# Middle mixture one expert further ahead, with two sum buffers and no loop, and the attention's mixture copied by VectorE

## The chip, the cores and the metric

The kernel runs on one core of one Trainium2 chip. The metric is the device time of one execution in microseconds, as the median over repeated runs of the same program; three runs of the kernel before are shown.

## What is computed

Sixteen sequences of 512 tokens with 256 features go through four blocks, each with a layer norm ahead of it and a residual around it: a linear-memory attention (layer 0), a mixture of eight routed experts and one shared expert (layer 0, the *middle mixture*), a windowed attention that is mixed with a state-space path and followed by an MLP (layer 1), and a top-1 mixture (layer 1). The change touches the second and the third:

```
# layer 0, mixture: 4 of 8 experts by grouped top-k, plus a shared expert
g = einsum('nh,ehi->eni', x, Wg);  u = einsum('nh,ehi->eni', x, Wu)
y = einsum('eni,eih->enh', silu(g) * u, Wd)
out = einsum('enh,ne->nh', y, cw) + mlp(x, Wg_s, Wu_s, Wd_s)
# layer 1, attention: gated sum of two products
x1 = x + g * (ao @ WO + bO) + (1 - g) * (states @ Cw)
```

Nothing of what is computed changes.

## The kernel before, in words

The program is written engine by engine: each engine has its own instruction list in program order, and engines meet at semaphores alone. The four blocks run one after another with a barrier between them. Matrix products are done in three parts (high x high, high x low, low x high halves; `three`, L70 to L74), so every operand of TensorE exists as a rounded high half and a remainder.

**Middle mixture** (`moe_phase`, L77, `shared=True`; its tiles are called `b_...`). A turn of the schedule is one expert of one sequence; nine experts make a sequence. In turn `e` TensorE does `down(e)` (L498: 12 matmuls of 256 columns into `y_ps`, one buffer) and then `gate_up(e + AHEAD)` (L486: 12 matmuls of 512 columns into one of the two slots of `gu_ps`), with `AHEAD = 2` (L86). Turns 2 and 3 have the transposes and the router of the next sequence as well. `down(e)` waits for the low half of `h` of expert `e` and for VectorE's sum of expert `e-1`, since `y_ps` has one buffer (two halves of it are signalled apart). `gate_up` waits until the slot that it overwrites was multiplied.

ScalarE's turn: `h_hi_copy(e)` (L254), `silu(e+1)` (L246), then parts of the next sequence. VectorE's turn: `h_lo_sub(e)` (L384), `accumulate(e-1)` (L392, four additions into the sum `acc`), `times_up(e+1)` (L375), then an extra part of the next sequence, by expert: 0 `stats_of` (L297), 1 `normalise` (L307), 4 `best_groups` (L332), 5 `lo_sub` (L370), 6 `ranks` (L316), 7 `weights_top4` (L345). The sum of the last expert ends the body. GpSimd only computes one inverse deviation per sequence.

SyncE's queue, per sequence `it` (L187 to L197): wait, load sequence `it+1` into the other half of `x_in`, wait for the whole sum of `it`, store `acc`. So the load of a sequence stands behind the store of the sequence two before it. `acc` has one buffer (L112); the first sum of a sequence waits for the store of the one before (L398).

`steps` (L56) runs the first and the last sequence as straight code and the fourteen between them in a hardware loop of seven turns of two sequences; there the values of waits and the DMA addresses come from registers.

**Layer-1 attention** (`attn1_phase`, L1306; tiles `c_...`) is straight code for all sequences. Per sequence 32 steps `n` run as a pipeline: scores (TensorE), `maxima` (VectorE, L1864), `exp` (ScalarE), inverse sums (VectorE), `normalise` (GpSimd), transposes (TensorE), `pT_copy` (ScalarE), values (TensorE). After each eight steps the product of a quarter is formed by `mix(it, t)` (L2115) in the PSUM tile `c_ps`, and `mix_copy(it, t)` (L1693, ScalarE) copies it to `mixed`, from which GpSimd builds `x1` in five parts (L1593 on). `mix(t+1)` and the next sequence's `state_input` (L2062) wait for that copy, because `c_ps` is one buffer. ScalarE's copies stand at `n` = 18, 26 and 34 and after the loop.

Of the kernel before, what the change touches and what calls it, by code (L numbers as in the profile page):

```python
# [51 lines left out]
def first_step(it):  # L52
    return isinstance(it, int) and it == 0


def steps(eng, body):  # L56

    body(0, 0)
    with eng.Fori(0, NSEQ // 2 - 1) as turn:
        body(turn * 2 + 1, 1)  # L60
        body(turn * 2 + 2, 0)
    body(NSEQ - 1, 1)


def sequence(v, it):
# [11 lines left out]
def moe_phase(nc, name, src, dst, wg_d, wu_d, wd_d, gate_d, bias_d, lower_d, half_d, ident_d, shared):  # L77
# [5 lines left out]
    NT = 1 if shared else 2  # L83
    YB = T * D // SEQ
    BT = T // YB
    AHEAD = 2  # L86
    src_v = src.rearrange("(n t p) d -> n p t d", t=T, p=P)
    dst_v = dst.rearrange("(n t p) d -> n p t d", t=T, p=P)
    with ExitStack() as ctx:
# [19 lines left out]
        eps = sb("eps", [P, T])  # L109
        ident = sb("ident", [P, P])  # L110
        x_in = sb("x_in", [P, 2, T, D])
        acc = sb("acc", [P, T, D])  # L112
        xn = sb("xn", [P, T, D])
        xT = sb("xT", [P, DC, SEQ])
        xT_hi = sb("xT_hi", [P, 2, DC, SEQ], F32R)
# [44 lines left out]
        hlo_ready = sem("hlo_ready")  # L160
        y_ready = sem("y_ready")
        acc_done = sem("acc_done")
        stored = sem("stored")
        dve_order = sem("dve_order")
        pool_order = sem("pool_order")
        LOADS = 8 if shared else 7
# [7 lines left out]
        @block.sync  # L174
        def _(sp):
            sp.dma_start(x_in[:, 0], src_v[0]).then_inc(x_loaded, 16)
            sp.dma_start(wgu_raw[:, 0, :], wg_d.rearrange("p e c i -> p (e c i)")).then_inc(loaded, 16)
            sp.dma_start(wgu_raw[:, 1, :], wu_d.rearrange("p e c i -> p (e c i)")).then_inc(loaded, 16)
            sp.dma_start(wd_raw[:], wd_d.rearrange("p e d -> p (e d)")).then_inc(loaded, 16)
            sp.dma_start(gate[:], gate_d).then_inc(loaded, 16)  # L180
            sp.dma_start(lower[:], lower_d).then_inc(loaded, 16)
            sp.dma_start(half[:], half_d).then_inc(loaded, 16)
            sp.dma_start(ident[:], ident_d).then_inc(loaded, 16)
            if shared:
                sp.dma_start(bias[:], bias_d).then_inc(loaded, 16)

            def body(it, par):  # L187

                if not last_step(it):

                    sp.wait_ge(var_ready, it + 1)
                    if not first_step(it):
                        sp.wait_ge(acc_done, (it - 1) * T * E + T)
                    sp.dma_start(x_in[:, 1 - par], sequence(src_v, it + 1)).then_inc(x_loaded, 16)

                sp.wait_ge(acc_done, (it + 1) * T * E)
                sp.dma_start(sequence(dst_v, it), acc[:]).then_inc(stored, 16)  # L197

            steps(sp, body)
            sp.wait_ge(stored, 16 * NSEQ)  # L200

        @block.gpsimd
        def _(pool):
# [14 lines left out]
        def _(act):  # L218
# [49 lines left out]
                evacuate(0, 1)  # L268
            hi_copy(0, 0)
            silu(0, 0, 0)  # L270

            def body(it, par):
                for e in range(E):
                    h_hi_copy(it, par, e)
                    if e + 1 < E:
                        silu(it, par, e + 1)
                    elif not last_step(it):
                        silu(it + 1, 1 - par, 0)
                    if not last_step(it):
                        if e == 2:  # L280
                            evacuate(it + 1, 0)
                        if e == (3 if shared else 4):
                            scores(it + 1)
                        if e == (4 if shared else 5):
# [7 lines left out]
        def _(dve):  # L292
# [99 lines left out]
            def accumulate(it, par, e):  # L392
                for t in range(T):
                    if t % BT == 0:
                        dve.wait_ge(y_ready, (it * E + e) * YB + t // BT + 1)

                    if e == 0 and t == 0 and not first_step(it):
                        dve.wait_ge(stored, it * 16)  # L398

                    if e and t == 0:  # L400
                        dve.wait_ge(acc_done, (it * E + e) * T)
                    into = x_in[:, par, t, :] if e == 0 else acc[:, t, :]
                    if e < E0:
                        nc.vector.tensor_tensor(acc[:, t, :], y_ps[:, t, :], into, ALU.add).then_inc(acc_done, 1)
                    else:
                        nc.vector.scalar_tensor_tensor(acc[:, t, :], y_ps[:, t, :], cw[:, par, t, e - E0:e - E0 + 1], into, ALU.mult, ALU.add).then_inc(acc_done, 1)  # L406

            stats_of(0, 0)
            normalise(0, 0)
# [11 lines left out]
                weights_top1(0, 0)  # L421
            lo_sub(0, 0)
            times_up(0, 0, 0)

            def body(it, par):
                order.step(it)
                for e in range(E):
                    h_lo_sub(it, par, e)
                    if e:
                        accumulate(it, par, e - 1)  # L430
                    if e + 1 < E:
                        times_up(it, par, e + 1)
                    elif not last_step(it):
                        times_up(it + 1, 1 - par, 0)
                    if not last_step(it):
                        if e == 0:
                            stats_of(it + 1, 1 - par)
# [868 lines left out]
def attn1_phase(nc, x, out, wqk_d, wvg_d, bw_d, cw_d, wo_d, w1_d, w2_d, spread_d, cols_d, rows_d, b1_d, a_d, window_d, half_d, ident_d):  # L1306
# [7 lines left out]
    with ExitStack() as ctx:  # L1314
# [325 lines left out]
        def _(act):  # L1640
# [49 lines left out]
                after(act, pv_done, G - 1)  # L1690
                nc.scalar.copy(pT[:, n % 2, :, b[0]:2], t_ps[:, n % 2, :, b[0]:2]).then_inc(pT_ready, 1)  # L1691

            def mix_copy(it, t):  # L1693
                act.wait_ge(mix_in_psum, it * T + t + 1)
                after(act, x1_done, it * T + t)
                nc.scalar.copy(mixed[:], c_ps[:]).then_inc(mix_copied, 1)

            def ao_hi(it, t):
                act.wait_ge(pv_done, it * NS + (t + 1) * PAIRS1)
                after(act, mix_in_psum, it * T + t)  # L1700
# [39 lines left out]
            def body(it):  # L1740
                q4_copy(it, HELD)
                for n in range(NS + LAG_T):
                    if HELD + 1 + n < PAIRS1:
                        q4_copy(it, HELD + 1 + n)
                    if n < NS:
                        exp(it, n)
                    if n >= LAG_T:
                        pT_copy(it, n - LAG_T)
                    if n in (13, 21, 29):
                        ao_hi(it, (n - 13) // 8)  # L1750
                    if n == 10:
                        state_hi(it)
                    if n in (18, 26, 34):
                        mix_copy(it, (n - 18) // 8)
# [5 lines left out]
                mix_copy(it, T - 1)  # L1760
                if not last_step(it):
                    projections(it + 1)

# [20 lines left out]
        def _(dve):  # L1784
# [87 lines left out]
            def inverse_sums(it, n):  # L1872
                dve.wait_ge(exp_ready, it * NS + n + 1)
                after(dve, norm_ready, it * NS + n - 3)
                nc.vector.reciprocal(inv[:, n % 4], psum[:, n % 4]).then_inc(inv_ready, 1)  # L1875

            def ao_lo(it, t):
                dve.wait_ge(aohi_ready, it * T + t + 1)
                nc.vector.tensor_tensor(aoT_hl[1][:], oT[t], aoT_hl[0][:].bitcast(F32), ALU.subtract).then_inc(aolo_ready, 1)
# [55 lines left out]
            def body(it):  # L1935
# [3 lines left out]
                for n in range(NS + 1):  # L1939
# [894 lines left out]
```

## Time and profile before

| | us |
|---|---|
| median of 3 runs | 4768.33 |
| the three runs | 4777.87, 4767.22, 4768.33 |
| the profiled execution, its own time | 4779.36 |
| its span in the trace | 4777.4 |
| its mean granted clock of TensorE | 0.95 |

The profiled execution is 11 us above the median, and 2 us of its time lie outside the traced span. The middle mixture runs from about 1840 to 2659 us of the span and the layer-1 attention from about 2660 to 4415 us. Times in rows are from the start of the span. In the trace PE is TensorE's matmul, PEld its weight load, DVE is VectorE, ACT ScalarE, POOL GpSimd, SPq the queue of SyncE; L406 is line 406. Matmuls overlap: the end shown of one is later than the start of the next, so "idle" is counted from a modelled end.

### The profile page before, as it was taken

What the parts mean: (1) busy time and instruction counts of PE and PEld (TensorE: products, weight loads), DVE (VectorE), ACT (ScalarE), POOL (GpSimd) and SP (SyncE); (2) the same over time, 40 slices, a digit from 0 to 9 for tenths busy, and PEclk for the clock granted to TensorE, in tenths of its full rate; (3) what the DMA queues carried; (4) which work ended last, traced back from release to release, by engine and by line L of the source; (5) the groups of instructions that cost most, each with busy time, mean ns of one, the idle gap of its engine ahead of it and who ended that gap; (6) DMA issues with size and microseconds to landing.
All of it is one profiled execution on the core that took longest, in us unless ns stands there. A gap on an engine that the chain in (4) does not pass through costs nothing. (4 is left out here: it accounts for less than half of the span.)

```text
span 4777.4 us, 147918 instructions
## 1 busy us (share of the span) xinstructions
PE 4059.4 (85%) x60532; PEld 3227.1 (68%) x60628; DVE 2999.0 (63%) x7236; ACT 2449.4 (51%) x5553; POOL 2220.0 (46%) x2255
## 2 busy tenths in 40 slices
PE   3888898888888885888888599999999999998668
PEld 2776677677767775777777366666676666666656
DVE  2777777777776775777777555555555555554455
ACT  3545555555555442333333366666666666666335
POOL 4666666666666650000000155555554555555354
PEclk8999999999999997999999799999999999999669
DMA  2222222221222121000000211111111111110233
GB/s 82 56 48 57 67 48 52 66 60 46 53 67 58 44 48 49 27 18 18 27 18 22 78 28 28 28 28 28 28 31 31 46 28 28 28 28 23 101 125 111
DMA packets 173293, 221.53 MB, mean 46 GB/s; under 512 B 32349, under 2 KB 117472, under 8 KB 171232
## 3 DMA queue, kind: packets, MB, share of 16 engines
q1 hardware_dynamic: 166160, 195.49, 15.5%
q0 software_dynamic: 6480, 16.92, 1.0%
q8 instruction: 461, 7.55, 0.7%
q14 instruction: 192, 1.57, 0.1%
HBM read 68.35 MB, written 44.19 MB: 24 GB/s over the span
## 5 line engine op out<-in xcount | busy, mean ns | idle before, releaser
L1591 POOL TENSOR_TENSOR c_prob<-c_prob,c_inv 128x512 f32<-128x512 f32 (+1 forms) x512 | 482.6, 947 | 648.8 <-DVE c_inv L1875 639.1
L1680 ACT ACTIVATE c_prob<-c_s_ps,c_nmax 128x256 f32<-128x256 f32 (+1 forms) x1024 | 459.2, 464 | 156.6 <-DVE c_nmax L1870 155.3
L1870 DVE TENSOR_REDUCE c_nmax<-c_s_ps 128x2 f32<-128x512 f32 (+1 forms) x512 | 316.8, 619 | 265.9 <-PE c_s_ps L2080 263.6
L848 POOL TENSOR_TENSOR a_swap<-a_swap,a_sin 128x512 f32<-128x512 f32 x128 | 204.9, 1600 | 533.0 <-DMA a_swap<-a_raw 533.0
L212 POOL TENSOR_TENSOR b_var<-b_mv,b_eps 128x4 f32<-128x4 f32 x16 | 8.5, 533 | 696.6 <-DVE b_mv L304 696.5
L889 ACT COPY a_raw<-a_w_ps 128x512 f32<-128x512 f32 x256 | 150.3, 587 | 332.1 <-PE a_w_ps L74 331.7
L1691 ACT COPY c_pT<-c_t_ps 128x512 f32<-128x512 f32 (+1 forms) x512 | 280.5, 551 | 50.0 <-PE c_ab_ps L2112 49.9
L2092 PE MATMUL c_t_ps<-c_ident,c_prob 128*128 128x128 f32 x1792 | 284.6, 275 | 21.8 <-ACT c_pT L1691 16.1
L1170 PE MATMUL a_w_ps<-a_mem,a_sT 64*32 64x65 f32 x14848 | 216.1, 226 | 94.7 <-issue 91.2
L2092 PEld LDWEIGHTS c_t_ps<-c_ident,c_prob 128*128 128x128 f32 x1792 | 214.5, 141 | 101.4 <-POOL c_prob L1591 36.2
L2080 PE MATMUL c_s_ps<-c_k,c_q 128*128 128x512 f32 (+1 forms) x512 | 272.6, 532 | 3.5 <-ACT c_prob L1680 3.5
L252 ACT ACTIVATE b_s_sb<-b_gu_ps 128x512 f32<-128x512 f32 x144 | 86.1, 598 | 368.9 <-PE b_gu_ps L74 368.9
L1170 PEld LDWEIGHTS a_w_ps<-a_mem,a_sT 64*32 64x32 f32 x14848 | 170.2, 106 | 146.2 <-issue 125.1
L72 PE MATMUL b_y_ps<-b_wd_hi,b_h_hi 128*128 128x256 f32 x576 | 176.6, 307 | 94.4 <-DVE b_acc L406 47.3
L72 PE MATMUL a_w_ps<-a_xT_hi,a_wqk_hi 128*128 128x512 f32 x512 | 233.3, 456 | 20.2 <-DVE a_x_ln L968 12.2
L1911 DVE TENSOR_TENSOR c_hT_lo<-c_ff,c_hT_hi 128x512 fp32r<-128x512 f32 x128 | 88.6, 692 | 248.6 <-ACT c_hT_hi L1725 248.6
L72 PE MATMUL b_gu_ps<-b_xT_hi,b_wgu_hi 128*128 128x512 f32 x576 | 234.1, 406 | 10.7 <-DVE b_xT_lo L373 10.7
L73 PE MATMUL b_gu_ps<-b_xT_hi,b_wgu_lo 128*128 128x512 f32 x576 | 232.9, 404 | 0.0
L74 PE MATMUL b_gu_ps<-b_xT_lo,b_wgu_hi 128*128 128x512 f32 x576 | 230.2, 400 | 0.0
L1680 ACT ACTIVATION_READ_ACCUMULATOR c_prob<-c_s_ps,c_nmax 128x1 f32 x1024 | 223.0, 218 | 0.0
L73 PE MATMUL a_w_ps<-a_xT_hi,a_wqk_lo 128*128 128x512 f32 x512 | 216.9, 424 | 3.0 <-issue 3.0
L74 PE MATMUL a_w_ps<-a_xT_lo,a_wqk_hi 128*128 128x512 f32 x512 | 215.9, 422 | 3.0 <-issue 3.0
(407 smaller groups left out, 13508.9 us busy)
## 6 DMA issues: line engine op xcount, KB each, us to landing
a_swap<-a_raw SPq DMA_DIRECT2D x1024, 64.0 KB
c_k<-c_aoT_hi SPq DMA_DIRECT2D x86, 128.0 KB, 2.4
c_k<-c_aoT_lo SPq DMA_DIRECT2D x86, 128.0 KB, 2.4
c_k<-c_stage SPq DMA_DIRECT2D x84, 128.0 KB, 2.3
d_xb<-sorted_rows SPq DMA_DIRECT2D x71, 130.0 KB
a_x_ln<-x SPq DMA_DIRECT2D x128, 64.0 KB, 2.1
a_acc<-x SPq DMA_DIRECT2D x64, 128.0 KB
after_attn<-a_acc SPq DMA_DIRECT2D x64, 128.0 KB, 2.5
```

What stands on the lines that cost most here:

```text
L72: nc.tensor.matmul(out, w[0], x[0], start=start, stop=False, **options)
L73: nc.tensor.matmul(out, w[1], x[0], start=False, stop=False, **options)
L74: return nc.tensor.matmul(out, w[0], x[1], start=False, stop=stop, **options)
L848: nc.gpsimd.tensor_tensor(q_sw, q_sw, table(sin), ALU.mult)
L889: (rawq_ready, rawk_ready)[a].by(nc.scalar.copy(raw[:, m % 3, a], bank))
L1170: ins = nc.tensor.matmul(into[s * SEG:(s + 1) * SEG, r, j], sT[d, (n // T * T + j) % (2 * PU), a, tok], mem[d, s, j], start=True, stop=True)
L1591: nc.gpsimd.tensor_tensor(p, p, inv[:, n % 4].unsqueeze(2).to_broadcast([P, 2, KB])[:, :, keys_of(i)], ALU.mult).then_inc(norm_ready, 1)
L1680: last = nc.scalar.activation(prob[:, n % 4, h, keys_of(i)], s_ps[:, n % 2, h, keys_of(i)], ACT.Exp, bias=nmax[:, n % 4, h:h + 1], accum_o ...
L1691: nc.scalar.copy(pT[:, n % 2, :, b[0]:2], t_ps[:, n % 2, :, b[0]:2]).then_inc(pT_ready, 1)
L1870: nc.vector.tensor_reduce(nmax[:, n % 4], s_ps[:, n % 2, :, keys_of(i)], AX.X, ALU.max, negate=True).then_inc(max_ready, 1)
L2080: last = nc.tensor.matmul(s_ps[:, n % 2, :, keys_of(i)], q4[:, j, i * P:(i + 1) * P], k4[:, j, :, keys_], start=False, stop=True, skip_gro ...
L2092: last = nc.tensor.transpose(t_ps[:, n % 2, h, b], prob[:, n % 4, h, b * P:(b + 1) * P], ident[:])
```

## The change

In the middle mixture experts run three ahead in TensorE's order. ScalarE's and VectorE's turn `e` handles the high and low half of expert `e+1` and the activation and product of expert `e+2`; VectorE adds the sum of `e-1` ahead of them. The sum has two buffers, each with a store semaphore of its own, and the sixteen sequences are written out as straight code. (`moe_phase` is called once, for this block.)

```
-    body(0, 0)
-    with eng.Fori(0, NSEQ // 2 - 1) as turn:
-        body(turn * 2 + 1, 1)
-        body(turn * 2 + 2, 0)
-    body(NSEQ - 1, 1)
+    for it in range(NSEQ):
+        body(it, it % 2)
...
-    AHEAD = 2
+    AHEAD = 3
...
-        acc = sb("acc", [P, T, D])
+        acc = sb("acc", [P, 2, T, D])
...
-                sp.dma_start(sequence(dst_v, it), acc[:]).then_inc(stored, 16)
+                sp.dma_start(sequence(dst_v, it), acc[:, par]).then_inc(stored[par], 16)
...
             def body(it, par):
                 for e in range(E):
-                    h_hi_copy(it, par, e)
-                    if e + 1 < E:
-                        silu(it, par, e + 1)
-                    elif not last_step(it):
-                        silu(it + 1, 1 - par, 0)
+                    for stage, later in ((h_hi_copy, e + 1), (silu, e + 2)):
+                        if later < E:
+                            stage(it, par, later)
+                        elif not last_step(it):
+                            stage(it + 1, 1 - par, later - E)
...
-                    if e == 0 and t == 0 and not first_step(it):
-                        dve.wait_ge(stored, it * 16)
+                    if e == 0 and t == 0 and it >= 2:
+                        dve.wait_ge(stored[par], it // 2 * 16)
...
                 for e in range(E):
-                    h_lo_sub(it, par, e)
                     if e:
                         accumulate(it, par, e - 1)
-                    if e + 1 < E:
-                        times_up(it, par, e + 1)
-                    elif not last_step(it):
-                        times_up(it + 1, 1 - par, 0)
+                    for stage, later in ((h_lo_sub, e + 1), (times_up, e + 2)):
+                        if later < E:
+                            stage(it, par, later)
+                        elif not last_step(it):
+                            stage(it + 1, 1 - par, later - E)
```

In the layer-1 attention `mix_copy` moves from ScalarE's list to VectorE's, at `n` = 18 and 26 and, after the loop, around the last low half:

```
-            def mix_copy(it, t):
-                act.wait_ge(mix_in_psum, it * T + t + 1)
-                after(act, x1_done, it * T + t)
-                nc.scalar.copy(mixed[:], c_ps[:]).then_inc(mix_copied, 1)
...
+            def mix_copy(it, t):
+                dve.wait_ge(mix_in_psum, it * T + t + 1)
+                after(dve, x1_done, it * T + t)
+                nc.vector.tensor_copy(mixed[:], c_ps[:]).then_inc(mix_copied, 1)
...
+                    if n in (18, 26):
+                        mix_copy(it, (n - 18) // 8)
...
+                mix_copy(it, T - 2)
                 ao_lo(it, T - 1)
                 if more:
                     qk_lo(it + 1, 0, 1)
+                mix_copy(it, T - 1)
                 stats2_of(it, T - 2)
```

## Rows read from the trace of the kernel before

**Rows 1.** Busy us of PE, PEld, DVE, ACT, POOL by stretch; clock, DMA share, GB/s.

```profile
1884.00:2656.00 772.00, 676.64 (x3793) 577.24 (x3792) 557.91 (x1643) 240.18 (x361) 23.43 (x30) 0.97 0.07 20
2740.00:4370.00 1630.00, 1522.85 (x10526) 1112.57 (x10619) 896.87 (x2074) 1083.96 (x3134) 876.90 (x1044) 1.00 0.12 30
```

**Rows 2.** Groups by line, 1884 to 2656 us: busy, mean ns, idle before and releasers.

```profile
L72 PE MATMUL b_y_ps<-b_wd_hi,b_h_hi 128*128 128x256 f32 x576 | 176.6, 307 | 94.4 <-DVE b_acc L406 47.3 <-DVE b_acc L404 39.6 <-DVE b_h_lo L390 7.5
...
L300 DVE BATCH_NORM_STATS2 b_stats<-b_x_in 128x6 f32<-128x256 f32 x60 | 21.1, 414 | 42.8 <-DMA b_x_in<-after_attn 42.8
```

**Rows 3.** Who waited for whom, 1884 to 2656 us: total, times, longest.

```profile
PE b_y_ps L72 <- DVE b_acc L406: 47.3, 31, 2.2
PE b_y_ps L72 <- DVE b_acc L404: 39.6, 14, 3.3
DVE b_h_lo L390 <- issue: 8.8, 6, 1.6
```

**Rows 4.** Instructions of VectorE in time, in one middle sequence.

```profile
2177.87 1.41 DVE L300 BATCH_NORM_STATS2 b_stats<-b_x_in 128x6 f32<-128x256 f32 x4 [2.57 <-DMA b_x_in<-after_attn]
...
2179.61 0.66 DVE L390 TENSOR_TENSOR b_h_lo<-b_h_sb,b_h_hi 128x512 fp32r<-128x512 f32 x1
2180.18 1.41 DVE L404 TENSOR_TENSOR b_acc<-b_y_ps,b_x_in 128x256 f32<-128x256 f32 x4
...
2198.74 0.69 DVE L382 TENSOR_TENSOR b_h_sb<-b_s_sb,b_gu_ps 128x512 f32<-128x512 f32 x1 [1.62 <-ACT b_s_sb L252]
2199.35 0.18 DVE L336 TENSOR_TENSOR b_score_c<-b_score,b_bias 128x32 f32<-128x32 f32 x1
...
2202.16 0.69 DVE L390 TENSOR_TENSOR b_h_lo<-b_h_sb,b_h_hi 128x512 fp32r<-128x512 f32 x1
2202.77 1.65 DVE L406 SCALAR_TENSOR_TENSOR b_acc<-b_y_ps,b_cw,b_acc 128x256 f32<-128x256 f32 x4
...
2222.95 0.69 DVE L390 TENSOR_TENSOR b_h_lo<-b_h_sb,b_h_hi 128x512 fp32r<-128x512 f32 x1 [1.32 <-issue]
```

**Rows 5.** Instructions of TensorE in time, at the three kinds of pause.

```profile
2180.99 0.55 PE L72 MATMUL b_y_ps<-b_wd_hi,b_h_hi 128*128 128x256 f32 x1 [2.85 <-DVE b_acc L404]
...
2183.68 0.63 PE L72 MATMUL b_gu_ps<-b_xT_hi,b_wgu_hi 128*128 128x512 f32 x1
...
2203.69 0.39 PE L72 MATMUL b_y_ps<-b_wd_hi,b_h_hi 128*128 128x256 f32 x1 [1.44 <-DVE b_acc L406]
...
2205.27 0.40 PE L72 MATMUL b_gu_ps<-b_xT_hi,b_wgu_hi 128*128 128x512 f32 x1
...
2223.79 0.38 PE L72 MATMUL b_y_ps<-b_wd_hi,b_h_hi 128*128 128x256 f32 x1 [1.15 <-DVE b_h_lo L390]
```

**Rows 6.** DMA issues of SyncE in time, the store and the load of two sequences.

```profile
2173.05 0.39 SPq L197 DMA_DIRECT2D after_ffn<-b_acc  x1
2173.80 0.38 SPq L194 DMA_DIRECT2D b_x_in<-after_attn  x1
...
2221.66 0.39 SPq L197 DMA_DIRECT2D after_ffn<-b_acc  x1
2222.69 0.38 SPq L194 DMA_DIRECT2D b_x_in<-after_attn  x1
```

**Rows 7.** Granted clock in the stretch after the pause at 2178 us.

```profile
2181.00:2183.70 2.70, 2.70 (x13) 2.70 (x14) 2.70 (x8) 0.62 (x1) 0.41 (x1) 0.51 0.00 0
```

**Rows 8.** Groups of ScalarE and VectorE, 2740 to 4370 us: copies of 512 columns from PSUM.

```profile
L1696 ACT COPY c_mixed<-c_c_ps 128x512 f32<-128x512 f32 x60 | 35.8, 597 | 21.1 <-PE c_c_ps L74 21.1
...
L1850 DVE CAST c_aoT_lo<-c_ab_ps 128x512 fp32r<-128x512 f32 x25 | 17.2, 690 | 10.5 <-PE c_ab_ps L2052 7.6 <-DMA c_k<-c_aoT_lo 3.0
```

**Rows 9.** Instructions of VectorE in time, one attention sequence.

```profile
3193.72 0.69 DVE L1870 TENSOR_REDUCE c_nmax<-c_s_ps 128x2 f32<-128x512 f32 x1 [0.79 <-PE c_s_ps L2080]
...
3210.03 0.69 DVE L1870 TENSOR_REDUCE c_nmax<-c_s_ps 128x2 f32<-128x512 f32 x1 [0.79 <-PE c_s_ps L2080]
...
3226.94 0.69 DVE L1879 TENSOR_TENSOR c_aoT_lo<-c_ab_ps,c_aoT_hi 128x512 fp32r<-128x512 f32 x1 [4.73 <-ACT c_aoT_hi L1705]
```

**Rows 10.** Instructions of ScalarE in time, the last copy of the same sequence.

```profile
3229.99 0.59 ACT L1696 COPY c_mixed<-c_c_ps 128x512 f32<-128x512 f32 x1 [1.40 <-PE c_c_ps L74]
```

**Rows 11.** DMA queue of instruction fetches, 2740 to 4370 us: packets, MB, share.

```profile
q8 instruction: 87, 1.43, 0.4%
```

**Rows 12.** DMA issues of the page: count, KB each, median us to landing.

```profile
c_k<-c_stage SPq DMA_DIRECT2D x84, 128.0 KB, 2.3
```

More of the change, by code:

```diff
@@ L162, in moe_phase @@
         acc_done = sem("acc_done")
-        stored = sem("stored")
+        stored = [sem(f"stored{k}") for k in range(2)]
         dve_order = sem("dve_order")
@@ L196, in body @@
                 sp.wait_ge(acc_done, (it + 1) * T * E)
-                sp.dma_start(sequence(dst_v, it), acc[:]).then_inc(stored, 16)
+                sp.dma_start(sequence(dst_v, it), acc[:, par]).then_inc(stored[par], 16)
             steps(sp, body)
-            sp.wait_ge(stored, 16 * NSEQ)
+            for k in range(2):
+                sp.wait_ge(stored[k], 16 * NSEQ // 2)
         @block.gpsimd
@@ L270, in _ @@
             silu(0, 0, 0)
+            h_hi_copy(0, 0, 0)
+            silu(0, 0, 1)
             def body(it, par):
                 for e in range(E):
-                    h_hi_copy(it, par, e)
-                    if e + 1 < E:
-                        silu(it, par, e + 1)
-                    elif not last_step(it):
-                        silu(it + 1, 1 - par, 0)
+                    for stage, later in ((h_hi_copy, e + 1), (silu, e + 2)):
[3 more added lines that the diff above has]
+                            stage(it + 1, 1 - par, later - E)
                     if not last_step(it):
@@ L395, in accumulate @@
                         dve.wait_ge(y_ready, (it * E + e) * YB + t // BT + 1)
-                    if e == 0 and t == 0 and not first_step(it):
-                        dve.wait_ge(stored, it * 16)
+                    if e == 0 and t == 0 and it >= 2:
+                        dve.wait_ge(stored[par], it // 2 * 16)
                     if e and t == 0:
                         dve.wait_ge(acc_done, (it * E + e) * T)
-                    into = x_in[:, par, t, :] if e == 0 else acc[:, t, :]
+                    into = x_in[:, par, t, :] if e == 0 else acc[:, par, t, :]
                     if e < E0:
-                        nc.vector.tensor_tensor(acc[:, t, :], y_ps[:, t, :], into, ALU.add).then_inc(acc_done, 1)
+                        nc.vector.tensor_tensor(acc[:, par, t, :], y_ps[:, t, :], into, ALU.add).then_inc(acc_done, 1)
                     else:
-                        nc.vector.scalar_tensor_tensor(acc[:, t, :], y_ps[:, t, :], cw[:, par, t, e - E0:e - E0 + 1], into, ALU.mult, ALU.add).then_inc(acc_done, 1)
+                        nc.vector.scalar_tensor_tensor(acc[:, par, t, :], y_ps[:, t, :], cw[:, par, t, e - E0:e - E0 + 1], into, ALU.mult, ALU.add).then_inc(acc_done, 1)
             stats_of(0, 0)
@@ L423, in _ @@
             times_up(0, 0, 0)
+            h_lo_sub(0, 0, 0)
+            times_up(0, 0, 1)
             def body(it, par):
@@ L1752, in body @@
                         state_hi(it)
-                    if n in (18, 26, 34):
-                        mix_copy(it, (n - 18) // 8)
                     if n in (29, 32) and not last_step(it):
@@ L1759, in body @@
                     qk_hi(it + 1, 0, 1)
-                mix_copy(it, T - 1)
                 if not last_step(it):
```

## The prediction

> **What bounds the kernel now.** I read the busy time by stretch first. In both stages that the change touches TensorE is the busiest engine; in the middle mixture it is busy for 676.6 of 772 us, so 95 us at most can be won there without taking work off it, and in the attention for 1522.9 of 1630 us at full clock [rows 1]. VectorE, at 558 us, has room on average, so what matters is when it is late. The groups by line then put nearly all of TensorE's idle time ahead of one instruction, the first matmul of `down`: 94.4 us, and name three releasers [rows 2]. The waits give their number [rows 3]: 14 pauses end with the first sum of a sequence (39.6 us), 31 with a later sum (47.3 us); the rest, 7.5 us, falls on loop edges, where VectorE itself sits some 1.5 us (8.8 in 6) without a wait that the profile shows.
>
> The timeline says why [rows 4, 5]. Of the later sums, two per sequence are late: VectorE has `best_groups` (2199.35 to 2202.16, 2.81 us) or `ranks` (about the same) between `times_up` and the low half of the next expert, then `h_lo_sub` (0.61 us to the next start), then the sum that `down` waits for. TensorE idles 1.44 us there. The first sum is late because `stats_of` waits for the next sequence's rows (42.8 us of VectorE in all [rows 2]); that load is issued behind the store of the sequence before, 0.75 us after it within a loop turn and 1.03 us after it across an edge [rows 6]. This pause also lowers TensorE's clock: in the 2.7 us after it the granted clock is 0.51, the 1.2 GHz level [rows 7], and `down` takes 2.69 us (2180.99 to 2183.68) where after the short pause it takes 1.58 (2203.69 to 2205.27) [rows 5]. In seven of the 14 it runs like this and in two about half as far; in the other five it kept its speed, among them all three whose pause was 2.03 to 2.23 us.
>
> **The change part by part.**
>
> *Three ahead, VectorE's new order.* No instruction is added. `y_ps` still has one buffer, so `down(e+1)` still waits for the sum of `e`, and the extra part still stands ahead of that sum. `times_up` now takes expert `e+2`, but TensorE finishes that gate-up right before `down(e)`, so it starts no earlier against `down` than it did. What changes in the late path is one piece: `h_lo_sub` is done before `times_up` and the extra part, and no longer between them and the sum. That is 0.61 us (2202.16 to 2202.77) [rows 4]. So the two routing pauses shrink by 0.6 us each and do not go: 30 of them in 15 sequences, **18 us**. What is late next is the same sum, behind the same extra part. The bounds are 0.45 us (VectorE starts the turn late from the extra before) and 0.75 us: 14 to 23 us.
>
> *The pause at the start of a sequence.* `stats_of` to the first sum loses its `h_lo_sub` too, 0.57 us (2179.61 to 2180.18) [rows 4]. The DMA itself stays: its place in SyncE's queue is unchanged. In straight code its issue can follow the store's 0.39 us plus a few hundredths instead of 0.75, a gain of 0.3 us, and of 0.6 at the edges [rows 6]. The eight pauses that don't follow an edge average 3.12 us; 3.12 - 0.57 - 0.3 leaves 2.25. Fourteen of these are 31 us in place of 39.6 + 7.5 = 47.1 us with the edges [rows 2]: **16 us**. The load may not land earlier for being issued earlier, since the store is still moving (bound: 0.3 us less each, 4 us), or as much as 0.5 us earlier (3 us more).
>
> *The clock.* A pause of 2.25 us lies beside those that kept their speed. Seven full losses of 1.1 us in `down`, two of half that, and some 0.3 us in each gate-up behind the seven are 11 us; I take **10 us** back, with bounds 0 and 11.
>
> *No loop.* The six edges are in the 47.1 us above. The nearest rows for straight code are those of the attention: 21,145 matmuls and weight loads of TensorE in 1630 us, with 87 fetch packets [rows 1, 11]. That is 13 in a microsecond where the mixture has 9.8, so I cost the longer code at nothing.
>
> *Two sum buffers.* The first sum waits for x, not for the store: VectorE's idle time ahead of `stats_of` is put down to the load [rows 2], and the sum follows without a gap [rows 4]. Nothing is won or lost.
>
> *The tail.* In the last sequence no gate-up is left between the last three `down`; one more sum is exposed, **+1 us**.
>
> *The copies in the attention.* 64 copies leave ScalarE (597 ns) and come to VectorE, whose nearest row is its copy of the same shape from PSUM, 690 ns [rows 8]. At `n` = 18 and 26 VectorE stands idle for 0.79 us ahead of the next `maxima`, waiting for TensorE [rows 9]; the product is in PSUM by then because `mix` precedes those scores in TensorE's order, and 0.61 us of occupancy fit. The third falls into 4.73 us of idle time [rows 9]. The fourth waits for TensorE on ScalarE already (1.40 us [rows 10]) and will on VectorE; queued behind it are a statistic and the next low half, whose input comes later. ScalarE's relief of 0.5 us is not on a path: at these places TensorE is busy and `exp` waits for `maxima`. I take **0**, with 64 x 0.09 = +6 us (each copy longer and felt) and 32 x 0.25 = -8 us (each early `exp` felt) as ends.
> The Trainium skill (Perfetto Trace Analysis, "Optimizing Scalar/DVE Operations") speaks against this move: it puts the access to PSUM at about 125 ns for VectorE and 51 ns for ScalarE. By it the copy costs 74 ns more, 5 us for 64; the rows' 93 ns agree in sign, and neither enters the sum while idle time covers the copy.
>
> *Sum:* 18 + 16 + 10 - 1 = 43 us, 4779.4 - 43 = 4736 for the profiled execution, which stands 11 us above the median; against the median, **4725 us**. About 0.3% (14 us) is what a measurement of this kernel can tell from no change.
>
> **The rivals.**
>
> *The load eats it.* If the load lands when it does now, the pause at the start of a sequence stays near 2.8 us and the clock still falls. Left are 18 us, the edges' 8 and minus 1: 4743 us. For it: store and load are 512 KB each and moving at once. Against: at edges the load is issued 0.3 us later, and there edge and first pause together are longer by more than that. 0.17.
>
> *The look-ahead covers all routing.* If VectorE gets through `best_groups` and `ranks` before the sum is due, the remaining 30 x 1.0 us go too: 4695 us. For it: VectorE's average load. Against: the order above; `times_up(e+2)` still waits for a gate-up that ends as `down(e)` starts. 0.10.
>
> *The copies block `maxima`.* VectorE's list is strict, and a copy that is late holds the next `maxima`, `exp` and transposes. If the idle time is no cover, 64 x 0.69 = 44 us come back and the time is unchanged, 4769 us. Against: the idle times of rows 9. 0.07.
>
> *Straight code must be fetched (slower than before).* The attention fetched 87 packets [rows 11] for some 27,400 instructions [rows 1], 315 each; the mixture's 9,600 are 31 packets. If each stops an engine on the path for 2.3 us (what the attention's small transfers take to land [rows 12]), that is 71 us: 4768 - 43 + 71 = 4796 us. It turns the sign from 43 / 31 = 1.4 us per packet, and an edge with its refilled queue costs VectorE 1.32 us now [rows 4]. Against: the attention runs so without it. 0.05.
> The Trainium skill (Runtime: NRT & Kernel Launch, "Instruction fetch mechanics") says that straight code is fetched ahead and that a taken branch breaks this; by that rule this rival falls, and the 1.32 us at an edge [rows 4] agrees with its second half. No row here shows the first half for this stage.
>
> **How the numbers follow.** My forecast has 0.61. Its own bounds: 14 to 23, 12 to 19 and 0 to 11 us, less 1, and -6 to +8 for the attention; not all at one end at once, so 4710 to 4740. The range takes in the load rival above and reaches part of the way to the look-ahead below: 4701 to 4747 leaves out some 0.2. Faster by over 0.3%: 0.61 + 0.17 + 0.10 = 0.88; within 0.3%: 0.07; slower: 0.05.
>
> **What would show it.** In the changed profile the idle time ahead of `down` should be about 31 us by the first sum (14 waits near 2.2 us) and 30 by later sums (pauses near 0.9 us), with none from `h_lo` and no loop edge on VectorE; the second `down` of a sequence should take about 1.5 us at full clock; a middle sequence 45.6 us, where it is 48.6 now (store to store [rows 6]). The attention's sequence should stay at 107 us and the copies read about 690 ns. I am wrong on the order if the routing pauses vanish or keep 1.4 us, on the load if the first pause stays above 2.7, and on the copies if `maxima` waits for them.

## The result and the profile after

| | before | after |
|---|---|---|
| median, runs of both taken together, us | 4773.1 (4 runs) | 4715.08 (4 runs, 4709.93 to 4737.31) |
| ratio after to before, 95% interval | | 0.9895 (0.9866 to 0.9924) |
| profiled execution, own time / span | 4779.36 / 4777.4 | 4714.08 / 4712.3 |
| mean granted clock | 0.95 | 0.95 |

The kernel became faster by 1.05%, between 36 and 64 us by the interval; 4725 was predicted, in a range of 4701 to 4747.

First the stages. The busy times by stretch of the kernel after (columns as in [rows 1]):

```profile
1877.00:2602.00 725.00, 663.41 (x3793) 568.43 (x3791) 555.78 (x1643) 243.58 (x361) 18.09 (x30) 0.98 0.07 22
2685.00:4305.00 1620.00, 1519.42 (x10526) 1111.60 (x10620) 933.57 (x2134) 1056.32 (x3075) 875.26 (x1044) 1.00 0.12 30
```

The counts of TensorE's instructions in the two stretches are those of [rows 1], so the stretches compare: the mixture's is 47 us shorter, 34 of it TensorE's idle time (95.4 to 61.6 us) and 13 its busy time. The stretch of the attention is 10 us shorter; 60 instructions have come to VectorE and 59 left ScalarE.

Where TensorE's idle time stands, in the groups by line and then in the waits, both of 1877 to 2602 us:

```profile
L69 PE MATMUL b_y_ps<-b_wd_hi,b_h_hi 128*128 128x256 f32 x576 | 169.6, 294 | 60.2 <-DVE b_acc L404 33.9 <-DVE b_acc L406 26.3
...
L390 DVE TENSOR_TENSOR b_h_lo<-b_h_sb,b_h_hi 128x512 fp32r<-128x512 f32 x144 | 97.9, 680 | 1.4 <-ACT b_h_hi L258 1.4
```

```profile
DVE b_stats L300 <- DMA b_x_in<-after_attn: 37.6, 14, 3.4
PE b_y_ps L69 <- DVE b_acc L404: 33.9, 14, 3.1
PE b_y_ps L69 <- DVE b_acc L406: 26.3, 32, 0.9
```

Against [rows 2, 3]: 94.4 us are 60.2. The 14 first sums are still late (39.6 to 33.9 us); the later sums are late as often as before, for half as long (47.3 to 26.3 us, the longest 0.9); the low half and the loop edges are gone as a cause.

Both pauses in time, first VectorE (an extra part, a sum; then the start of a sequence), then TensorE:

```profile
2141.81 0.42 DVE L330 TENSOR_REDUCE b_rank<-b_wins 128x32 f32<-128x256 f32 x1
2142.26 1.66 DVE L406 SCALAR_TENSOR_TENSOR b_acc<-b_y_ps,b_cw,b_acc 128x256 f32<-128x256 f32 x4
2143.84 0.68 DVE L390 TENSOR_TENSOR b_h_lo<-b_h_sb,b_h_hi 128x512 fp32r<-128x512 f32 x1
...
2155.93 1.41 DVE L300 BATCH_NORM_STATS2 b_stats<-b_x_in 128x6 f32<-128x256 f32 x4 [2.60 <-DMA b_x_in<-after_attn]
...
2157.68 1.38 DVE L404 TENSOR_TENSOR b_acc<-b_y_ps,b_x_in 128x256 f32<-128x256 f32 x4
2158.98 0.68 DVE L390 TENSOR_TENSOR b_h_lo<-b_h_sb,b_h_hi 128x512 fp32r<-128x512 f32 x1
```

```profile
2143.29 0.36 PE L69 MATMUL b_y_ps<-b_wd_hi,b_h_hi 128*128 128x256 f32 x1 [0.85 <-DVE b_acc L406]
...
2158.54 0.36 PE L69 MATMUL b_y_ps<-b_wd_hi,b_h_hi 128*128 128x256 f32 x1 [2.34 <-DVE b_acc L404]
```

In [rows 4] a low half lay between the extra part and the sum. Now the sum begins where `ranks` or the statistics end, and the low half comes behind it.

The queue of SyncE at one start of a sequence, and the load's line in the DMA issues of the mixture:

```profile
1921.33 0.38 SPq L194 DMA_DIRECT2D after_ffn<-b_acc  x1
1921.81 0.45 SPq L191 DMA_DIRECT2D b_x_in<-after_attn  x1
```

```profile
b_x_in<-after_attn SPq DMA_DIRECT2D x14, 512.0 KB, 4.8
```

The same line of the kernel before (1884 to 2656 us):

```profile
b_x_in<-after_attn SPq DMA_DIRECT2D x14, 512.0 KB, 4.5
```

The load is issued 0.48 us behind the store, where [rows 6] show 0.75 and 1.03. But it takes 4.8 us to land, by the median, where it took 4.5. VectorE's statistics start as it lands. In eight sequences no loop edge lay between store and load, and there the statistics start 5.29 us after the end of the last sum, before and after: the earlier issue bought no earlier landing. In the six where an edge lay between, they start after 5.41 us in place of 6.09.

TensorE's clock, at a sequence start with a pause of 2.44 us and a matmul or two of each part (two stretches by window, then TensorE in time):

```profile
2111.62:2113.60 1.98, 1.98 (x12) 1.98 (x13) 1.98 (x6) 0.00 (x0) 0.58 (x1) 0.70 0.00 0
2113.70:2117.40 3.70, 3.70 (x13) 2.89 (x13) 3.09 (x8) 0.62 (x1) 0.00 (x0) 0.71 0.00 0
```

```profile
2111.62 0.35 PE L69 MATMUL b_y_ps<-b_wd_hi,b_h_hi 128*128 128x256 f32 x1 [2.44 <-DVE b_acc L404]
2111.81 0.28 PE L70 MATMUL b_y_ps<-b_wd_hi,b_h_lo 128*128 128x256 f32 x1
...
2113.01 0.41 PE L69 MATMUL b_y_ps<-b_wd_hi,b_h_hi 128*128 128x256 f32 x1
...
2114.50 0.63 PE L71 MATMUL b_gu_ps<-b_xT_lo,b_wgu_hi 128*128 128x512 f32 x1
...
2116.05 0.39 PE L69 MATMUL b_gu_ps<-b_xT_hi,b_wgu_hi 128*128 128x512 f32 x1
```

The clock still falls at a sequence start. `down` begins at the 2.4 GHz level (0.28 us a matmul), is at 1.2 GHz by its end (0.41), and the gate-up behind it stays there until 2116 us (0.63 a matmul, then 0.39). The clock falls like this, in `down` or in the gate-up behind it, at 7 of the 14 starts. Before it was 10: in seven of them `down` ran at 1.2 GHz from about its first matmul on, in two for about half of it, and once, behind a pause of 3.33 us, only the gate-up was slow (1.49 and 4.34 us). I took the time from the first matmul of each `down` to the first matmul of the gate-up behind it, and that gate-up's time likewise: `down` fell from 2.18 to 1.74 us on average (1.49 at full clock), the gate-up from 3.46 to 3.31 us (2.80 at full clock).

The copies, by tile (shortest, median and longest in ns, first and last start), and two lines of the waits of 2685 to 4305 us, who waits for them and whom they wait for:

```profile
L1874 DVE COPY c_mixed<-c_c_ps x64: 668/680/693, 2706.0 to 4347.7; 128x512 f32<-128x512 f32 x64
```

```profile
POOL c_t L1597 <- DVE c_mixed L1874: 77.6, 30, 3.1
...
DVE c_mixed L1874 <- PE c_c_ps L71: 35.3, 30, 1.7
```

A copy takes 680 ns in place of 597 [rows 8]; the third and the fourth of each sequence (30 in 15) wait for the product, the first two find it ready. Last, the two queues of instruction fetches in the mixture (packets, MB, share), after and then before:

```profile
q8 instruction: 30, 0.49, 0.3%
q14 instruction: 23, 0.19, 0.1%
```

```profile
q14 instruction: 35, 0.29, 0.1%
q8 instruction: 7, 0.11, 0.1%
```

The straight code fetches 0.68 MB in place of 0.40. The Trainium skill (Runtime: NRT & Kernel Launch, "Instruction fetch mechanics") says that the next page is fetched while the current one executes. The trace agrees: the waits of 1877 to 2602 us list no idle time of VectorE, ScalarE or TensorE's matmuls that ends without a releaser (VectorE had 8.8 us of it with the loop [rows 3]), and the 30 routing pauses all lie between 0.78 and 0.86 us, so no packet shows as a stop.

### The profile page after: what moved, and what is told of

Its sections match the earlier page's. It is cut to its first block and busy times, and to the rows that moved or that the text cites. A ratio compares the mean times of both kernels' runs of the same rounds, so it can differ in the third digit from the quotient of the medians.

```text
span 4712.3 us, 146646 instructions
## 1 busy us (share of the span) xinstructions
PE 4049.5 (86%) x60532; PEld 3223.5 (68%) x60628; DVE 3044.9 (65%) x7300; ACT 2423.9 (51%) x5489; POOL 2208.2 (47%) x2255
## 3 DMA queue, kind: packets, MB, share of 16 engines
q14 instruction: 178, 1.46, 0.1%
## 5 line engine op out<-in xcount | busy, mean ns | idle before, releaser
L406 DVE SCALAR_TENSOR_TENSOR b_acc<-b_y_ps,b_cw,b_acc 128x256 f32<-128x256 f32 x512 | 211.9, 476 | 23.0 <-PE b_y_ps L71 22.0
L69 PE MATMUL b_y_ps<-b_wd_hi,b_h_hi 128*128 128x256 f32 x576 | 169.6, 294 | 60.2 <-DVE b_acc L404 33.9
```

What stands on the lines that cost most here:

```text
L69: nc.tensor.matmul(out, w[0], x[0], start=start, stop=False, **options)
L406: nc.vector.scalar_tensor_tensor(acc[:, par, t, :], y_ps[:, t, :], cw[:, par, t, e - E0:e - E0 + 1], into, ALU.mult, ALU.add).then_inc(acc ...
```

## The experiments

My theory after this: the idle time in the mixture comes from two places in VectorE's order, the load behind the store and the extra part ahead of a sum; the change removes a low half from both, the straight code removes the edges, and the rest of the change is worth nothing. Rivals: the loop is the whole gain; the second sum buffer pays; the copies pay or cost. Three ahead and the new orders of ScalarE and VectorE were not run apart.

**The mixture alone, and the attention alone.** The first has the whole change of `moe_phase` and `steps` and ScalarE's copies, the second the kernel before with VectorE's copies.

```
# mixture alone: kernel after, but in attn1_phase
-            def mix_copy(it, t):
-                dve.wait_ge(mix_in_psum, it * T + t + 1)
+            def mix_copy(it, t):
+                act.wait_ge(mix_in_psum, it * T + t + 1)
...
# attention alone: kernel before, but the other way round
```

> The change's mixture, with the attention's copies left on ScalarE. My theory (the whole gain is the mixture's, the copies are worth nothing): the time of the changed kernel within 6 us, 45 to 52 us under before; the mixture from its first gate-up to its last sum takes 732 us as in the changed profile; a quiet attention sequence takes 106.9 to 107.2 us as in both profiles. Rival (the copies give the 10 us by which the attention was shorter in the changed profile): 10 us slower than the changed kernel, and every attention sequence about 0.7 us longer than in the changed one.

Measured: 4720.56 us, ratio 0.9916 (0.9892 to 0.994). The mixture took 732.6 us, and a quiet attention sequence 106.9 to 107.0 us, so not every sequence became longer.

> The mixture of before, with the attention's copies on VectorE alone. My theory: the time of before within 6 us; no sequence of the attention gains, its three long sequences of 110 us in the profile of before come and go by themselves. Rival (the copies give 10 us): 10 us faster than before, with no sequence above 108 us.

Measured: 4768.68 us, ratio 1.0003 (0.9985 to 1.002). The mixture carries the gain; of the copies the totals show nothing over 0.2%. The profiles say a little more, at the end of this section.

**Straight code alone.** The kernel before with its sixteen sequences written out.

```
-    body(0, 0)
-    with eng.Fori(0, NSEQ // 2 - 1) as turn:
-        body(turn * 2 + 1, 1)
-        body(turn * 2 + 2, 0)
-    body(NSEQ - 1, 1)
+    for it in range(NSEQ):
+        body(it, it % 2)
```

> The kernel of before with the mixture's loop written out as straight code, and nothing else. My theory: the six edge pauses (7.5 us) go and the load follows its store sooner; the sum of the edge and first-sum pauses falls from 47 to about 40 us, the clock still falls after them, the routing pauses stay at 1.44 us: 5 to 12 us faster than before. Rival (the register instructions of the loop are what costs, and straight code is most of the gain): 30 to 50 us faster. Rival (straight code must wait for its fetches): slower than before.

Measured: 4758.07 us, ratio 0.9979 (0.9959 to 0.9998): 12 us below the kernel before by the medians, 1 to 20 by the interval. Its waits in the mixture:

```profile
PE b_y_ps L69 <- DVE b_acc L403: 45.4, 31, 2.3
...
PE b_y_ps L69 <- DVE b_acc L401: 40.4, 14, 3.6
```

The edges are gone (they were 7.5 us [rows 2]), and 40.4 us at the first sums stand for 39.6; the routing pauses stay. The first `down` of a sequence still runs slowly, in 13 of 14.

**Further ahead, in the loop.** The new orders and three ahead, VectorE's copies, but the loop and one sum buffer.

```
# kernel after, but
-    for it in range(NSEQ):
-        body(it, it % 2)
+    body(0, 0)
+    with eng.Fori(0, NSEQ // 2 - 1) as turn:
+        body(turn * 2 + 1, 1)
+        body(turn * 2 + 2, 0)
+    body(NSEQ - 1, 1)
...
-        acc = sb("acc", [P, 2, T, D])
+        acc = sb("acc", [P, T, D])
```

> Three ahead with VectorE's and ScalarE's new order, but the loop kept and one sum buffer. My theory: the routing pauses fall from 1.44 to 0.83 us (30 of them, 18 us), the first-sum pauses by 0.57 each (8 us) and part of the clock comes back (0 to 10 us); the edges stay: 25 to 37 us faster than before. Rival (the loop hides the look-ahead, or one sum buffer makes the first sum wait for the store): under 15 us faster.

Measured: 4738.19 us, ratio 0.9937 (0.9917 to 0.9957), 31 us below the kernel before. Its waits:

```profile
PE b_y_ps L72 <- DVE b_acc L406: 36.5, 14, 3.5
PE b_y_ps L72 <- DVE b_acc L408: 28.6, 30, 1.1
...
DVE b_h_lo L392 <- issue: 10.3, 6, 1.9
```

VectorE still loses its 1.7 us at each edge (10.3 in 6), but TensorE no longer waits for that low half: it is now due a turn later. Looking ahead hides VectorE's edge. It does not hide SyncE's: across an edge the load is issued later, and the first sum behind it is later still. The queue at an edge, and the first `down` that waits, in a sequence without an edge and in the one behind this edge:

```profile
2222.62 0.39 SPq L197 DMA_DIRECT2D after_ffn<-b_acc  x1
2223.66 0.38 SPq L194 DMA_DIRECT2D b_x_in<-after_attn  x1
```

```profile
2184.76 0.39 PE L72 MATMUL b_y_ps<-b_wd_hi,b_h_hi 128*128 128x256 f32 x1 [1.99 <-DVE b_acc L406]
...
2231.61 0.58 PE L72 MATMUL b_y_ps<-b_wd_hi,b_h_hi 128*128 128x256 f32 x1 [3.48 <-DVE b_acc L406]
```

In the six sequences behind an edge the pause at the first sum averages 3.02 us, in the other eight 2.30. So an edge still costs TensorE 0.7 us there. What the straight code adds is the difference to the next kernel.

**One sum buffer.** The kernel after with `acc` and `stored` single.

```
-        acc = sb("acc", [P, 2, T, D])
+        acc = sb("acc", [P, T, D])
...
-                    if e == 0 and t == 0 and it >= 2:
-                        dve.wait_ge(stored[par], it // 2 * 16)
+                    if e == 0 and t == 0 and it >= 1:
+                        dve.wait_ge(stored, it * 16)
```

> The changed kernel with one sum buffer and one store semaphore, as before; straight code and three ahead stay. My theory: the first sum waits for the statistics, which wait for the load, and the store has landed over a microsecond earlier, so the second buffer is worth nothing: the time of the changed kernel within 5 us, first-sum pauses near 2.4 us. Rival (the second buffer lets the first sum start sooner): first-sum pauses of 3 us or more and 10 to 25 us slower than the changed kernel.

Measured: 4717.03 us, ratio 0.9904 (0.9883 to 0.9926). Its waits:

```profile
PE b_y_ps L69 <- DVE b_acc L403: 33.2, 14, 3.0
PE b_y_ps L69 <- DVE b_acc L405: 24.8, 30, 0.9
...
DVE b_acc L403 <- DMA after_ffn<-b_acc: 0.4, 1, 0.4
```

The sum waited once for a store, for 0.4 us. The second buffer is worth nothing. Against the kernel before it in this list, straight code saves 3.3 us at the first sums, 3.8 at the routing pauses (0.95 to 0.83 us each), and 6.7 us in the 14 first `down`s (their times add up to 30.9 and 24.2 us): 14 us of the stage's 747.9 and 733.8 us, from the first gate-up to the last sum. The 3.3 us come from the edges alone: without the loop the first pauses average 2.37 us, in the six sequences that stood behind an edge as in the others. Why the clock fell less often is not shown. I had put the loop's price beyond its edges at nothing.

**The load ahead of the store.** The load of sequence `it+2` is issued when the first sum of `it` has freed its half of `x_in`, long before the store of `it`.

```
-                if not last_step(it):
-                    sp.wait_ge(var_ready, it + 1)
-                    if not first_step(it):
-                        sp.wait_ge(acc_done, (it - 1) * T * E + T)
-                    sp.dma_start(x_in[:, 1 - par], sequence(src_v, it + 1)).then_inc(x_loaded, 16)
+                if it == 0:
+                    sp.wait_ge(var_ready, 1)
+                    sp.dma_start(x_in[:, 1], sequence(src_v, 1)).then_inc(x_loaded, 16)
+                if it + 2 < NSEQ:
+                    sp.wait_ge(var_ready, it + 2)
+                    sp.wait_ge(acc_done, it * T * E + T)
+                    sp.dma_start(x_in[:, par], sequence(src_v, it + 2)).then_inc(x_loaded, 16)
```

> The changed kernel, but SyncE issues the load of sequence it+2 as soon as the first sum of sequence it has freed its half of x_in, ahead of the store of it. My theory (the first-sum pauses are this load and nothing else): the 14 pauses of 2.4 us (33.9 us idle in the profile) fall under 0.3 us each and the clock no longer falls after them (some 4 us): 32 to 40 us faster than the changed kernel. Rival (VectorE's own work, statistics and first sum, is late anyway): pauses of 1 us or more stay, under 20 us faster.

Measured: 4665.74 us, ratio 0.9806 (0.9782 to 0.983). Of TensorE's waits for a sum one line is left:

```profile
PE b_y_ps L69 <- DVE b_acc L407: 25.8, 32, 0.9
```

```profile
1884.00:2550.00 666.00, 641.62 (x3737) 553.04 (x3736) 545.51 (x1621) 242.40 (x359) 18.16 (x30) 1.00 0.07 24
```

The first pauses are gone, all 14, and with them the falls of the clock (1.00 in the stage). Against the kernel with one sum buffer, which was timed beside it and does what the changed kernel does, this is 51 us less, more than the 33 us of first pauses and than the 32 to 40 that I expected: the 14 `down`s and gate-ups behind them took 72 us there and take 59 here. The place of one DMA in a queue set the pause: the load is now issued some 39 us before the statistics read it, and they no longer wait for it.

**The extra part ahead of the low half and the product.** Only `best_groups`, `ranks`, `weights_top4` and `lo_sub` move; in the loop over `e` of VectorE:

```
                     if e:
                         accumulate(it, par, e - 1)
+                    if not last_step(it):
+                        if e == 4:
+                            best_groups(it + 1)
...
                     for stage, later in ((h_lo_sub, e + 1), (times_up, e + 2)):
...
-                        if e == 4:
-                            best_groups(it + 1)
```

> The changed kernel, but VectorE does the routing parts of a turn (best_groups, lo_sub, ranks, weights_top4) right after accumulate and ahead of h_lo_sub and times_up, where it waits for ScalarE today. My theory (the routing pauses come from the place of these parts, between a wait for ScalarE and the sum): 30 pauses of 0.83 us fall to a third in total; 15 to 25 us faster than the changed kernel. Rival (VectorE is simply short of time in these turns): the pauses stay within 0.3 us of what they are.

Measured: 4688.56 us, ratio 0.9844 (0.9823 to 0.9865), 28 us below the kernel with one sum buffer, where I expected 15 to 25. Its waits:

```profile
PE b_y_ps L69 <- DVE b_acc L404: 34.8, 14, 3.4
...
PE b_y_ps L69 <- DVE b_acc L406: 1.4, 2, 0.9
```

All 30 routing pauses go, where I expected a third to stay; the two that are left are the tail's. `times_up` waits for ScalarE's activation anyway; the extra part now fills that wait instead of following it. At the sequence starts the clock falls oftener than in the changed kernel (11 of 14, `down` 2.21 us on average), though the pauses there are about as long; without that the gain would have been larger.

**Both.** The load's order of the one, and VectorE's extra parts ahead of the low half and the product, here all of them, the statistics and the normalising too (the expectation names only the routing parts).

> The load early and the routing parts first together. My theory: the two add up, 47 to 65 us faster than the changed kernel, near 4655 us where the changed one is at 4715; TensorE's idle time ahead of the down products falls from 60 to under 15 us. Rival (what one takes away the other meets: the pauses move to another place): no more than the better of the two.

Measured: 4636.76 us, ratio 0.9719 (0.9695 to 0.9744): 80 us below the kernel with one sum buffer, and the fastest here. The two parts add up (51 and 28), to more than the 47 to 65 us expected, and of the pauses ahead of `down` 1.4 us are left, in the tail. The busy times of its mixture:

```profile
1890.00:2520.00 630.00, 630.00 (x3708) 549.80 (x3708) 540.62 (x1617) 241.47 (x355) 23.41 (x30) 1.00 0.08 25
```

TensorE is busy for all of 630 us at full clock, and every sequence takes 40.7 or 40.8 us from store to store (45.0 to 47.6 in the changed kernel). What is left in this stage is TensorE's own work.

**The attention, again.** In the profiles so far the attention's stage, from the first sequence's fourth copy to the last sequence's, had been longer with ScalarE's copies. So three more profiles: the fastest kernel with ScalarE's copies, and both kernels of this study once more.

```
# the kernel of "Both", but in attn1_phase
-                dve.wait_ge(mix_in_psum, it * T + t + 1)
+                act.wait_ge(mix_in_psum, it * T + t + 1)
...
```

> The kernel of the run with both orders changed, but with the attention of the kernel before (ScalarE copies the mixture's products). Sixteen stages of attention from the first fourth copy to the last: 1610.9 to 1614.8 us in three profiles with ScalarE's copies, 1604.5 to 1608.6 in seven with VectorE's. If the copies set this (theory): 1610 us or more, at least three of the fifteen sequences above 107.6 us, and a median 4 to 10 us above 4636.8, so 4641 to 4647. If it is chance of the execution (rival): anywhere in 1604 to 1615, and the median within 3 us of 4636.8 as far as the runs can tell. The mixture stays as it was: sequences of 40.7 us, no pause but the tail's.

Measured: 4639.01 us, ratio 0.9725 (0.97 to 0.9749); stage 1611.0 us, three long sequences. The stage is as the theory asked, the median as the rival asked (within 3 us of 4636.8).

> The changed kernel, unchanged, for a second profile. If the copies set the length of the attention: 1604 to 1609 us as in the seven other profiles with VectorE's copies, at most four long sequences. If it is chance: 1604 to 1615. In the mixture the pause before the first sum of a sequence should average 2.3 to 2.5 us, with the second down at full clock in about eight of 14.

Measured: 4717.74 us; stage 1605.2 us, two long sequences. First pauses 33.5 us in 14, mean 2.39, with seven `down`s at full clock.

> The kernel before, unchanged, for a second profile. If the copies set the length of the attention: 1610 to 1615 us and at least three long sequences. If it is chance: 1604 to 1615. In the mixture the pause before the first sum should average 2.7 to 2.9 us, with about seven of 14 second downs at 2.7 us.

Measured: 4765.58 us; stage 1609.4 us, two long sequences, both just under what the theory asked for. First pauses 39.3 us in 14, mean 2.81, with six `down`s of 2.7 us.

With these, five profiles with ScalarE's copies have 1609.4 to 1614.8 us (mean 1612.0), eight with VectorE's 1604.5 to 1608.6 (mean 1606.1). The groups don't overlap, though by 0.8 us only, and both hold kernels with the old and with the new mixture, so I hold some 6 us for the copies' doing. The total times do not show it: 4639.0 against 4636.8 is less than the theory asked for, and with VectorE's copies alone the ratio was 1.0003. A quiet sequence takes 106.9 us in both. The difference lies in single sequences of up to 111 us. Over half of it is a pause ahead of the first scores of the next sequence, which wait for moves of the keys: TensorE waits for these 9.6 us on average in the five profiles with ScalarE's copies and 6.3 in the eight with VectorE's. In the kernel with both orders and ScalarE's copies, the waits of those scores read:

```profile
PE c_s_ps L2082 <- issue: 4.5, 7, 1.7
PE c_s_ps L2082 <- DMA c_k<-c_aoT_lo: 4.0, 6, 1.8
...
PE c_s_ps L2082 <- DMA c_k<-c_aoT_hi: 3.5, 5, 1.5
...
PE c_s_ps L2082 <- DMA c_k<-c_stage: 2.7, 2, 2.5
```

and in the changed kernel:

```profile
PE c_s_ps L2082 <- issue: 4.5, 10, 1.2
...
PE c_s_ps L2082 <- DMA c_k<-c_aoT_hi: 3.0, 6, 0.6
...
PE c_s_ps L2082 <- DMA c_k<-c_aoT_lo: 1.4, 3, 0.5
PE c_s_ps L2082 <- DMA c_k<-c_stage: 1.2, 2, 0.7
```

Why a key's move lands later when ScalarE copies stays open; no run here tells it apart.

## Why the prediction was right, and where it was off

The sum was 43 us. The mixture gave 47 us between the two profiles shown (779.6 to 732.2 us from the first gate-up to the last sum) and 44 between the second pair (776.3 to 732.3), the attention some 6. The idle time ahead of `down` reads 33.9 and 26.3 us where I had asked for 31 and 30, and a middle sequence takes 45.0 to 47.6 us where I had 45.6. By parts the 47 us are 13 at first sums and edges, 20 at the routing pauses, 1 in the tail, 8 by the clock, and 5 in the other `down`s and gate-ups, which no term of the sum had; 3 of these 5 come with straight code alone.

So the mechanism of the largest term held, and that the total came so near is in part luck: 3 us missing at the first sums and 2 at the clock are outweighed by 2 more at the routing pauses, 2 by the sign of the tail, and the 5 us of other matmuls and 6 of the attention that were not priced at all. One reading was wrong from the start. "95 us at most can be won" took TensorE's busy time for a floor, but that time holds the matmuls at 1.2 GHz, and the matmul ahead of a pause counts 0.39 us where without a pause the next one starts 0.23 us behind it. The kernel with both orders took 126 us off this stage (779.6 to 654.0 us) with the same matmuls.

- **Routing pauses, 18 us: right.** 30 pauses fell from 45.0 to 24.9 us, 20 us in all. From straight code alone to one sum buffer they fell from 43.1 to 24.8, 0.61 us each, which is the low half by [rows 4]. The other 2 us went with the loop: the seven pauses by `best_groups` in the first sequence of a loop turn were 1.64 to 1.68 us long and the others 1.45 on average, and without the loop all are alike (1.40 to 1.46); I hadn't counted that the loop reaches that far. That "the extra part still stands ahead of that sum" held: putting it elsewhere removed all 30.
- **First sums and edges, 16 us: measured 13.** 47.1 became 33.9, a mean of 2.42 where I had 2.25. The low half was worth what it was costed at: from the start of the statistics to the first sum it takes 1.74 us in place of 2.32 (costed 0.57). The step that failed is "a gain of 0.3 us" by the earlier issue in straight code: the load is issued 0.27 us earlier behind the store and takes 0.3 us longer, so without an edge the statistics start no sooner (5.29 us after the last sum, before and after). At the six edges they start 0.7 us sooner (6.09 to 5.41), which is more than the 0.6 that I gave to the issue. The lower bound named the failure, at 4 us.
- **The clock, 10 us: measured 8, on a wrong basis.** Against full clock the 14 `down`s lost 9.7 us before and 3.5 after, the 14 gate-ups behind them 9.2 and 7.1, by the averages above: 18.9 became 10.6. I had 11 us to get back, with "some 0.3 us in each gate-up"; behind the seven slow `down`s it was 0.8 on average, and six of the ten slow gate-ups cost 1 us and more. I had read `down` alone: one of the five that "kept its speed" had the fall in its gate-up. And "pause of 2.25 us lies beside those that kept their speed" fell: in the changed kernel a pause of 2.05 us was followed by a fall and one of 2.52 was not.
- **No loop, 0 beyond the edges; two buffers, 0; tail, -1:** the first was too low, and by the kernels in a loop and out of it part of what I gave to the orders belongs to it (a routing pause is 0.95 us in the loop and 0.83 outside). The buffer was 0. The tail has the wrong sign: it has one pause more, but its two pauses (0.88 and 0.51 us) stand for one of 2.25, so it gave 0.9 us.
- **The copies, 0, with ends of +6 and -8:** some -6 by the profiles, inside the ends by luck, from a place I had not looked at: I followed `maxima` and `exp`, and over half of it shows at the keys' moves. The copy's 680 ns, near the 690 I took, cost nothing.
- **The rivals.** The load did eat a part of one term, 3 us, not the clock with it. The look-ahead did not cover the routing. `maxima` was not held. The fetch rose to the 30 packets that the rival supposed, in the queue that it counted ([rows 11] leave out the other), and cost nothing visible.

The forecast was 10 us above the median that came: some 6 of it are the attention, if the profiles are right; the other 4 are what the mixture gave above the 43 in the pair of profiles shown (the second pair gave 44).

## What to carry to other kernels

Read a pause back to the instruction that stands in the way on its engine, and price the change by that instruction alone: moving 0.6 us of work from ahead of a late sum to behind it gave 0.6 us per pause, though the program looks a whole expert further ahead. Then ask what remains in the way: here one DMA behind another in a queue and an extra part ahead of a wait that it could have filled, and two moves of a few lines gave 80 us more, where the change itself gave some 50. Compare the issue and the landing of a transfer before counting an earlier issue as a gain, and follow a loop's edge on every engine's list, the DMA queue's too.

## What the runs showed of the hardware that was not expected

- The length of a pause alone does not decide whether TensorE's clock falls after it. In one profile, of the kernel with the copies alone, a `down` and its gate-up behind a pause of 3.29 us kept full speed (1.53 and 2.79 us, granted clock 1.00), and a `down` behind one of 2.04 us took 2.73 (0.50). A `down` at full speed does not prove that the clock stayed: in the kernel before, taken again, one took 1.51 us behind a pause of 3.33, and the gate-up behind it 4.34.
- How often the clock falls changed from kernel to kernel at pauses of about the same length: 14 first `down`s averaged 2.21 us with the routing pauses gone and 1.70 to 1.74 in four profiles with them, at pauses of 34.8 and 33.2 to 33.9 us in all. That the short pauses' going did it is not shown: in the loop, with short pauses, the average was 2.21 too, at 36.5 us. Part of a gain can go back in this way until the last long pause is gone; then the clock stayed at 1.00.
- A loop edge is felt on each engine's list by itself. VectorE loses 1.5 to 1.7 us at one (8.8 us in 6 [rows 3], 10.3 in 6 with the look-ahead), and TensorE no longer waits for that once the work behind it is due a turn later. But in the kernel with the look-ahead in the loop SyncE issues the load 0.3 us later across an edge, the load takes some 0.6 us longer to land, and TensorE's pause there is 3.02 us in place of 2.30. Why it takes longer stays open.
